# FP4 feed-forward in a four-layer block: levels by rounding the bit pattern on VectorE, the two lowest thresholds on GpSimd

## What is computed

```
_MID  = [0.25, 0.75, 1.25, 1.75, 2.5, 3.5, 5.0]
_GRID = [0.0, 0.5, 1.0, 1.5, 2.0, 3.0, 4.0, 6.0]
def fp4_quant_dequant(x):
    xb = x.reshape(shape[:-1] + (shape[-1] // BLOCK, BLOCK))
    scale = jnp.maximum(jnp.max(jnp.abs(xb), axis=-1, keepdims=True) / 6.0, 1e-12)
    xn = xb / scale
    idx = jnp.searchsorted(_MID, jnp.abs(xn))
    q = _GRID[idx] * jnp.sign(xn) * scale
def ffn(h, w_gate, w_up, w_down):          # widths 128 -> 352 -> 128
    gate = silu(fp4_linear(h, w_gate)); up = fp4_linear(h, w_up)
    return fp4_linear(gate * up, w_down)   # each fp4_linear quantises both operands
```

## Time and profile before

| | |
|---|---|
| time, median of 3 runs | 5523.27 us (5519.79 to 5526.17) |
| the profiled execution's own time | 5521.02 us |
| its span, first to last instruction | 5519.3 us |
| busy over the whole span | PE 4929.2, DVE 3922.5, ACT 3359.4, POOL 2660.5 us |
| stage of the FP4 feed-forward, weights' quantiser to last residual | from 569.95 to 917.75 us of the span |
| `qh` in it, VectorE, L738 | 16 instructions, mean 1908 ns |
| `qh` in it, GpSimd, L714 | 16 instructions, mean 1384 ns |

### The profile page before, as it was taken

One profiled execution on the slowest core, in us unless ns is written; L12 is line 12 of the kernel. 1 busy time (PEld: TensorE's weight loads), 2 busy tenths in 40 slices (PEclk: granted clock), 3 DMA queues, 4 the chain that ended last, 5 costly groups with the idle time before them and its releaser, 6 DMA issues. The chain is left out here.

```text
span 5519.3 us, 130512 instructions
## 1 busy us (share of the span) xinstructions
PE 4929.2 (89%) x50569; PEld 3352.3 (61%) x50569; DVE 3922.5 (71%) x6510; ACT 3359.4 (61%) x5923; POOL 2660.5 (48%) x1681
## 2 busy tenths in 40 slices
PE   6888555997899999999999999999999999799897
PEld 4444233554677667776777677766776777566544
DVE  5999797775677777777777677767777777477553
ACT  5776322554666666666666666666666666455444
POOL 4777110000566556665666566655555666266200
PEclk8999656998999999999999999999999999899898
DMA  2121000000000100010000000010001000000020
GB/s 84 61 77 62 4 0 7 2 1 19 17 12 12 29 14 11 11 30 15 11 11 20 25 11 11 12 30 12 11 11 33 12 11 11 14 2 2 24 62 19
DMA packets 76242, 113.90 MB, mean 21 GB/s; under 512 B 22496, under 2 KB 53424, under 8 KB 72048
## 3 DMA queue, kind: packets, MB, share of 16 engines
q1 hardware_dynamic: 67744, 110.60, 7.3%
q10 hardware_dynamic: 8256, 0.03, 0.1%
HBM read 70.38 MB, written 2.49 MB: 13 GB/s over the span
## 5 line engine op out<-in xcount | busy, mean ns | idle before, releaser
L2211 POOL TENSOR_TENSOR lt_qk<-lt_qk,lt_rot 128x1024 f32<-128x1024 f32 x384 | 907.0, 2362 | 207.3 <-DVE lt_rot L2575 207.3
L2221 POOL TENSOR_TENSOR lt_prob<-lt_prob,lt_total 128x1024 f32<-128x1024 f32 x192 | 365.1, 1902 | 1086.5 <-DVE lt_total L2597 1086.5
L2216 POOL TENSOR_TENSOR lt_qk<-lt_qk,lt_rnorm 128x1024 f32<-128x1024 f32 x384 | 726.2, 1901 | 110.5 <-ACT lt_rnorm L2451 102.9
L2258 PE MATMUL lt_ps<-lt_w_qk,lt_xs 128*128 128x512 f32 x1536 | 749.8, 611 | 23.0 <-DMA lt_scales<-in_L_scales 11.3
L2310 PE MATMUL lt_ps<-lt_z,lt_fold 128*128 128x256 f32 x3072 | 678.8, 379 | 1.3 <-ACT lt_z L2479 1.3
L2310 PEld LDWEIGHTS lt_ps<-lt_z,lt_fold 128*128 128x128 f32 x3072 | 583.6, 190 | 121.5 <-ACT lt_z L2479 24.4
L2572 DVE TENSOR_TENSOR lt_qk<-lt_ps,lt_table 128x1024 f32<-128x1024 f32 x384 | 467.8, 1218 | 79.0 <-ACT lt_sq L2441 72.1
L2575 DVE TENSOR_TENSOR lt_rot<-lt_ps,lt_table 128x512 f32<-128x512 f32 x768 | 490.1, 679 | 0.0
L2587 DVE TENSOR_REDUCE lt_nmax<-lt_ps 128x16 f32<-128x1024 f32 x192 | 229.9, 1197 | 360.5 <-PE lt_ps L2278 360.4
L2582 DVE TENSOR_REDUCE lt_norm<-lt_sq 128x16 f32<-128x1024 f32 x384 | 463.4, 1207 | 0.0
L2258 PEld LDWEIGHTS lt_ps<-lt_w_qk,lt_xs 128*128 128x128 f32 x1536 | 272.7, 193 | 253.9 <-issue 247.2
(11 more groups left out here) (406 smaller groups left out, 9935.5 us busy)
## 6 DMA issues: line engine op xcount, KB each, us to landing
mb_bs<-mb_rows SPq DMA_DIRECT2D x16, 1536.0 KB, 7.6
lt_xw<-lt_xw SPq DMA_DIRECT2D x192, 128.0 KB, 2.3
mb_bs<-mb_rows SPq DMA_DIRECT2D x16, 512.0 KB, 4.2
mo_gate_b<-mo_rows SPq DMA_DIRECT2D x16, 512.0 KB, 5.5
lt_xs<-h SPq DMA_DIRECT2D x96, 64.0 KB, 1.9
lt_w_qk<-in_L_ffn_Wqkv SPq DMA_DIRECT2D x6, 1024.0 KB, 4.9
lt_xs<-h SPq DMA_DIRECT2D x96, 63.8 KB, 1.9
lt_wvT<-in_L_wvT SPq DMA_DIRECT2D x6, 512.0 KB, 7.4
```

Source lines behind the costliest of these rows:

```text
L2211: pool.tensor_tensor(qk[:, u, :, :], qk[:, u, :, :], rot[:, u % 2, :, :], ALU.add).then_inc(sg["added"], 1)
L2216: pool.tensor_tensor(qk[:, u, :, :], qk[:, u, :, :], rnorm[:, u, :, :].to_broadcast([P, H, DH]), ALU.mult).then_inc(sg["qk"], 1)
L2258: last = pe.matmul(AT[u][:, 512 * k:512 * k + 512], xs[:, m.j, c:c + P], w_qk[:, a, 512 * k:512 * k + 512], start=True, stop=True)
```

## The change

The level is no longer counted with seven comparisons. On VectorE the scaled magnitude's exponent is cut out of its bits (a bitwise AND on the int32 view, writing `level`), a quarter of it less one unit in the last place is added to the magnitude (one multiply-and-add), and a second AND keeps sign, exponent and the first mantissa bit, which is the rounding to one mantissa bit. `mag` is now scaled to twice what it was (the reciprocal is taken of `half`, and waits for it), so this gives twice the level wherever the level is at least 1. Below that two thresholds decide, 0.25 and 0.75 (0.5 and 1.5 in the doubled scale): GpSimd compares `mag` with both into a new buffer `low`, adds the two with a third instruction, and VectorE's last level instruction takes max(level, 2) + low. These three GpSimd instructions stand ahead of the sign product, and need `mag` scaled.

```diff
-    STEPS = 11
+    STEPS = 6
...
     def pool(self, pool, n):
         sg, name = self.sg, self.name
+        pool.wait_ge(sg[name + "_scaled"], n + 1)
+        pool.sem_inc(sg[name + "_low_step"], 1)
+        pool.tensor_scalar(self.low[:, 0, :, :], self.mag[:, :, :], 1.5, -2.0, ALU.is_gt, ALU.add).then_inc(sg[name + "_lows"], 1)
+        pool.tensor_scalar(self.low[:, 1, :, :], self.mag[:, :, :], 0.5, None, ALU.is_gt).then_inc(sg[name + "_lows"], 1)
+        pool.wait_ge(sg[name + "_lows"], 2 * n + 2)
+        pool.tensor_tensor(self.low[:, 0, :, :], self.low[:, 0, :, :], self.low[:, 1, :, :], ALU.add).then_inc(sg[name + "_low"], 1)
         pool.wait_ge(sg[name + "_sign"], n + 1)
         pool.wait_ge(sg[name + "_half"], n + 1)
         pool.tensor_tensor(self.sign[:, :, :], self.sign[:, :, :], self.half[:, :, :].to_broadcast([P, self.blocks, 16]),
...
-        done(nc.vector.reciprocal(self.amax[:, :, :], self.scale[:, :, :]))
+        dve.wait_ge(sg[name + "_half"], n + 1)
+        done(nc.vector.reciprocal(self.amax[:, :, :], self.half[:, :, :]))
         dve.wait_ge(sg[name + "_mag"], n + 1)
-        done(nc.vector.tensor_tensor(self.mag[:, :, :], self.mag[:, :, :], self.amax[:, :, :].to_broadcast(shape), ALU.mult))
+        nc.vector.tensor_tensor(self.mag[:, :, :], self.mag[:, :, :], self.amax[:, :, :].to_broadcast(shape), ALU.mult).then_inc(sg[name + "_scaled"], 1)
+        dve.wait_ge(sg[name + "_scaled"], n + 1)
         yield
-        dve.wait_ge(sg[name + "_half"], n + 1)
-        done(nc.vector.tensor_scalar(flat(self.level), flat(self.mag), 5.0, 2.0, ALU.is_gt, ALU.mult))
+        bits = flat(self.level).bitcast(I32)
+        done(nc.vector.tensor_scalar(bits, flat(self.mag).bitcast(I32), 0x7F800000, None, ALU.bitwise_and))
         yield
-        for mid in (3.5, 2.5):
-            done(nc.vector.scalar_tensor_tensor(out=flat(self.level), in0=flat(self.mag), scalar=mid, in1=flat(self.level),
-                                                op0=ALU.is_gt, op1=ALU.add))
-            yield
-        done(nc.vector.tensor_scalar(flat(self.level), flat(self.level), 2.0, None, ALU.mult))
+        done(nc.vector.scalar_tensor_tensor(out=flat(self.level), in0=flat(self.level), scalar=0.25 - 2.0 ** -23, in1=flat(self.mag),
+                                            op0=ALU.mult, op1=ALU.add))
         yield
-        for mid in (1.75, 1.25, 0.75):
-            done(nc.vector.scalar_tensor_tensor(out=flat(self.level), in0=flat(self.mag), scalar=mid, in1=flat(self.level),
-                                                op0=ALU.is_gt, op1=ALU.add))
-            yield
-        nc.vector.scalar_tensor_tensor(out=flat(self.level), in0=flat(self.mag), scalar=0.25, in1=flat(self.level),
-                                       op0=ALU.is_gt, op1=ALU.add).then_inc(sg[name + "_level"], 1)
+        done(nc.vector.tensor_scalar(bits, bits, 0x7FC00000, None, ALU.bitwise_and))
+        yield
+        dve.wait_ge(sg[name + "_low"], n + 1)
+        nc.vector.scalar_tensor_tensor(out=flat(self.level), in0=flat(self.level), scalar=2.0, in1=self.low[:, 0, :, :].rearrange("p a b -> p (a b)"),
+                                       op0=ALU.max, op1=ALU.add).then_inc(sg[name + "_level"], 1)
```

More of the change, by code:

```diff
@@ L699, in __init__ @@
         self.level = sb(name + "_level", [P, blocks, 16])
+        self.low = sb(name + "_low", [P, 2, blocks, 16])
         self.blocks = blocks
```

## The result

The changed kernel takes 5540.42 us (median of 6 runs, 5532.84 to 5550.80), the kernel before 5519.19 (6 runs, 5512.45 to 5526.17). The ratio is 1.0039, 95% interval 1.0026 to 1.0052: slower, by 21 us. The forecast was 5495 and faster. The profiled execution took 5539.76 us. In experiment 4 one run of ten took 7406 us at a granted clock of 0.617, against about 0.95 in the others, and is left out of its ratio.

A forecast was written before the change was run, and what follows sets the result against it. Each item: 6.76 us over TensorE and ScalarE, then 11.76 on VectorE alone; only the latter can shrink. 5521.0 - 20.2 (16 items) - 2.3 (first two `qx`) - 3.7 (weights) = 5494.8, thus 5495; range 5480 to 5518.

The forecast's parts named there:

- the low end: GpSimd's comparisons in the quantiser: priced like one-input instructions, 0.77 us for 704 elements, 0.59 of it streaming.
- the upper bound taken from the two-input row: GpSimd's comparisons in the quantiser: at most the price of a two-input instruction, 1.38 us for 704 elements.
- the tail: In `qh`, from the scaling product's end to the end of `fp_hidq`: 7.4 us instead of 7.77.
- the weights: Weights quantised inside the norm before the first `qx`: norm ends earlier, `qx` starts at 600.65, -3.7 us.
- The fifth: Rival, GpSimd's comparisons: each operation a two-input pass, 2.77 and 1.38 us, +2.6 an item, 5536, slower; 8%.
- Rivals 1 to 4: Comparisons cost 1.38 us, 20%; no turns taken, 5%; AND at one element a cycle, 8%; TensorE's clock higher, 4%.
- Scaling product: In `qh`, VectorE's scaling of `mag` no longer meets GpSimd: 0.89 us instead of 1.91, -1.02 an item.
- Reciprocal behind `half`: In `qh`, VectorE's reciprocal must now wait for `half`: +0.13 us an item.
- some 2 us lost to GpSimd's four: Weights inside the norm: VectorE's time lost to the four GpSimd instructions, some 2 us.
- The way of the tokens behind the norm: Between norm and first `qx`: copy, transposes and ScalarE with wakes take 1.75 us, an estimate.
- the path over TensorE: From `fp_hidq` over the down product to the residual, TensorE and ScalarE: 6.76 us, hiding `qx`'s gain in the loop.
- the first two `qx`: Token quantisers with no `back` beside them: the gain of 1.15 us each counts there, -2.3 in all.

The follow-up runs named there:

- experiment 4: Changed kernel with the first GpSimd comparison made in one operation, its -2.0 left out; ratio 1.0024 to the kernel before, median 5530.97 us.
- experiment 3: Changed kernel with VectorE's wait for `low` moved ahead of its first AND, so VectorE idles while GpSimd compares and adds; one run, 5589.36 us.
- experiment 1: Changed kernel with GpSimd's two comparisons replaced by plain copies of `mag`, all waits kept; 5495.46 us, ratio 0.9955 to the kernel before.
- experiment 6: Kernel before with GpSimd's sign product waiting for the scaled `mag` instead of `half`; median 5508.91 us, ratio 0.9989 to the kernel before.
- experiment 5: Changed kernel with GpSimd's two comparisons replaced by copies in `qx` only; 5537.24 us, ratio 1.0040 to the kernel before.
- experiment 8: Changed kernel rounding the signed value on VectorE, with no GpSimd or ScalarE in the quantiser; 5421.51 us, ratio 0.9823 to the kernel before.

## Why the prediction was wrong

**The step that failed** is the price of GpSimd's tensor-scalar: "I take the low end, since the affine select also has one input and a comparison". That was 0.77 us for 704 elements; alone they take 1.97 with one operation and 2.57 with two (experiment 3). Both lie above the upper bound taken from the two-input row, 1.38, so the bracket itself was too narrow, and the range up to 5518 with it. Copies in their place, with every wait kept, bring the tail from 9.92 back to 7.57 us (experiment 1), so this one number carries the error in the item. Of the 6.8 us error in the weights it carries 4.7, the difference between the changed kernel's part and that with copies. The Trainium skill, "GPSIMD Engine Reference", section 7 (the notes under its table of pitfalls), would by its two rates for a compare-and-select body have given an estimate of 0.60 or 1.19 us of streaming; experiment 3 has 850 and 1970 ns at 256 and 704 elements, 2.5 ns an element, or 1.76 us for 704. The measurement decides.

**The rivals.** The fifth, slower, is what happened, and had been given 8%: its point of decision was 3.9 us for the two comparisons together, they take 4.5 alone and 4.9 in place, and its 5536 is near 5540. Its reason, a full pass for each operation, is not what experiment 4 shows. Rivals 1 to 4 are out: the comparisons are dearer than a two-input instruction; turns are taken (experiment 6); the ANDs take 0.53 us, so they keep the double rate; the clock stayed at 0.61 over the items, as before. The clock differed behind the stage, where no rival looked (the result, above).

**The item, step by step.** Scaling product 1.91 to 0.89: right. Reciprocal behind `half`: +0.13, as seen in the tokens and the hidden alike. Tail: forecast 7.4, measured 9.92. From the end of the scaling product to that of the second comparison the forecast had 2.47 us, and it was 5.06 (669.78 to 674.84): 2.6 us, the whole of the error. From there to `fp_hidq` it had 4.44, or 4.94 with its allowance of 0.5 for handovers, and it was 4.86, with L758 held until the sign product had ended, as forecast. In the first half the forecast was wrong in kind as well: VectorE's steps should have alternated with the comparisons; they ran beside the first one, and lay covered.

**The weights.** Forecast -3.7, measured +3.1. Besides the price, "some 2 us lost to GpSimd's four" was mis-sized because I counted only the quantiser's own steps as meeting GpSimd. The norm's L290 meets it too and lost 9.1 us. With copies the weights' part is 32.9 us, with the thresholds on VectorE 32.7, both some 1.6 less than before and not 3.7. The way of the tokens behind the norm was forecast well, 1.75 us against an idle of 1.57 ahead of the first `qx`; the norm's end was put too early.

**`qx` and the path over TensorE.** Right: the residual comes 6.76 us behind `fp_hidq` (659.92 to 666.68) as before, and a cheaper `qx` gives nothing (experiment 5). In the changed kernel `qx` itself gained nothing to waste: it takes 5.8 us instead of 5.7 and ends at 666.44, 0.24 us ahead of L298. So the 2.3 us that the forecast took from the first two `qx` did not come either; with copies `qx` takes 4.8, which is 0.9 us less, where the forecast had 1.15.

## What to carry to other kernels

An instruction moved to an engine whose row the trace lacks needs an upper bound by its arithmetic, not by how many inputs it has: here, at 256 elements, a comparison with a constant cost GpSimd 0.85 us and one with an addition behind it 1.07, against 0.42 for a copy and 0.62 for a product of two tensors. Look at what is queued in front of the moved work's consumers on that engine, and at which stretch of a pipeline the removed work lay in; only one of the two quantisers of each item counted. And before giving work away, look for fewer operations: a sum and a difference with a large multiple of the value's own power of two replaced threshold counting, absolute value, sign and sign product together (experiment 8).

## What the runs showed of the hardware

- GpSimd, f32: a comparison with a constant takes 0.85 us at 256 elements, 1.97 at 704 and 3.07 at 1120; with an addition behind it 1.07, 2.57 and 4.00 (experiment 3; at 1120 the norm's instructions waited beside them, at 256 and 704 VectorE was idle). A copy of 256 takes 0.42 (experiment 5).
- VectorE's bitwise AND on an int32 view of 704 elements takes 0.53 us (L750, L755), as long as a multiplication by a constant in f32 (L747 before, 0.527).
- VectorE's L290, a multiply-and-add with two per-partition operands that takes 0.41 us, waits for a GpSimd instruction like one with two tensor inputs does, for up to 3.2 us beyond its own length (L290 beside L715 in the weights, 3.60 us).
- Waiting was not always for the whole instruction. While GpSimd compared 704 elements (669.98 to 672.90), VectorE's L752 took 1.34 us instead of 0.89 and L755 its 0.53 us; in experiment 1 L752 took the same 1.34 us beside a copy of only 1.02, so that the longer comparison did not hold it longer than the copy. But at 256 elements L755 waited for the comparison's end (0.51 instead of 0.29), and in the weights L290 waited through all of 1120 elements. The Trainium skill, "SBUF — State Buffer", section "Who interferes with whom", has the loser blocked for the whole instruction; that fits L738, L758 and L290, not L752 and L755 at 704 elements. When in a comparison the port is held was not tried and stays open.
